# Two transformer layers on one core: neighbouring stages run into each other at the borders of attention, and the barriers between stages wait by part of the memory

## The chip, the cores and the metric

The kernel runs on one core of a Trainium2 chip. The metric is the device time of one execution in microseconds. TensorE is called PE here, with its weight loads as PEld, VectorE DVE, ScalarE ACT, GpSimd POOL, and SyncE SP; SP issues nearly all DMAs.

## The reference

The input x is 2 batches of 1024 tokens of 512 numbers, in float32. Six stages follow, each adding to x what it computes from a normalised x:

```python
x = x + 0.5 * L0_ffn(layernorm(x))   # hidden 1536, weights rounded to fp8, scales per column
x = x + L0_attn(layernorm(x))        # 16 query heads, 4 key/value heads of 32, biases, rope, causal
x = x + 0.5 * L0_ffn(layernorm(x))
x = x + 0.5 * L1_ffn(layernorm(x))   # hidden 2048
x = x + L1_attn(layernorm(x))        # 16 heads of 32, causal
x = x + 0.5 * L1_ffn(layernorm(x))
```

A feed-forward stage is `down(silu(gate(h)) * up(h))`; an attention stage is q, k, v, the causal softmax of q k / sqrt(32), times v, and the output projection.

## The kernel before

x stays in SBUF as 16 tiles of 128 tokens, and a chunk `c` is four tiles. Products in full precision are made from a high and a low part of each operand, in two or three passes. The stages are s = 0 to 5, of the kinds f0, a0, f0, f1, a1, f1.

**One plan sets every order.** `make_plan()` writes one list of steps, such as `("gu", s, g, c, m)` (gate and up products of one block of 128 hidden columns, group g, chunk c), `("down", s, g, c, i)` (down product of one token tile), `("ln_stats" / "ln_norm" / "ln_tp" / "ln_lo", s, t)` (the norm of tile t: statistics on DVE and POOL, the normalised tile `tmp` on ACT, four transposes on PE, high part on ACT, low part on DVE), `piece` and `piece_out` (256 tokens of q or k of four heads), `stack` (three DMAs that stack the parts of one head's q or k for the score products), `row` (scores by query, for the row maxima), `m_tp` and `m_lo` (the maxima transposed and sent by two `mrow` DMAs into the stacked q), `key` (scores by key), `pv` (times v), `take`, `y_turn`, `y_fin`, `y_tp` (the heads' results turned into `yT`), `oproj` (output projection). Each engine's program walks the same list and issues its share of each step in that order, with waits on semaphores that earlier steps raise; no engine reorders anything. Helper objects of the class `Beside` interleave jobs (norms, weights) with the main steps, one piece of a job at each `tick`. The PSUM bank of each step is chosen from the plan by `bank_turns`.

**A feed-forward stage** (`ffn`) loops over groups g (4 of f0, 8 of f1) and the four chunks. A chunk has MTS gate/up steps: three for f0 (16 products of 512 columns each) and two for f1 (24 products each). The down steps of a chunk, four tiles of six products, come one chunk later. `silu`, `prod` and the high part `a` are made by ACT and DVE, the low part by `a_lo` on DVE. In f0, down results go through `dso` (DVE) and are added to x by POOL; in f1, DVE adds them.

**An attention stage** (`attention`) first makes eight pieces (q and k of the first four heads), then the eight stacks, the v products, and 13 row steps ahead of the first key step; after that, row, key and pv steps and the products of the next heads run interleaved.

**Borders.** Between stages stands a step `begin`, at which ACT, DVE, POOL and SP each wait until all of x is complete, because the tiles of the new stage lie on memory of the old one:

```python
def begin(s):
    if s:
        on.wait_ge(*x_done(s - 1, NT - 1))
        all_kept(on)
```

SP's `begin` also issues small loads after that wait: three scale loads for f0; two rope tables, three bias columns and `bo` for a0. PE has no `begin`; it waits for what each step reads. `w_read` says when a weight's place may be overwritten.

The borders between feed-forward and attention are called A (stage 0 to 1, at 299 to 356 us of the span), B (1 to 2, at 804 to 844), C (3 to 4, at 1614 to 1666) and D (4 to 5, at 2157 to 2203).

## Time and profile before

| what | value |
|---|---|
| median of 3 runs | 2704.14 us (2702.6 to 2717.95) |
| the profiled execution | 2707.04 us, span 2705.3 us |
| PE busy | 2620.1 us, 97% of the span |
| DVE, ACT, POOL busy | 1368.5, 1078.1, 637.4 us (51%, 40%, 24%) |
| TensorE's clock, mean | 0.993 of 2.4 GHz |

The chip's profiler recorded one execution. Busy times don't add up to the span, since the engines work side by side; only the time in which PE has no work, or works at half clock, can be read as a loss where PE is the engine that everything ends on. Times in the text are microseconds from the start of the span.

### The profile page before, as it was taken

The page shows a single profiled execution, that of the slowest core. Times are in us where ns is not written, and L with a number is a line of the kernel's source. Part 1 is how long each engine was busy: PE and PEld are TensorE (multiplying, and loading weights), DVE is VectorE, ACT ScalarE, POOL GpSimd, SP SyncE. Part 2 cuts the span into 40 slices and gives each one's busy share as a digit, 9 for nine tenths or more (in the row PEclk, how much of TensorE's full clock was granted, in tenths as well). Part 3 has the DMA queues.
Part 4 walks back from the last instruction along what each step waited for, and adds up shares of the span by engine and source line. Part 5 has one row for each costly group of instructions (what it writes and reads, how often), then busy time and mean ns, then how long its engine had stood idle before and what let it go on. Part 6 is the DMA issues. An engine that isn't in the chain of part 4 may idle for free.

```text
span 2705.3 us, 36133 instructions
## 1 busy us (share of the span) xinstructions
PE 2620.1 (97%) x13216; PEld 1999.4 (74%) x13216; DVE 1368.5 (51%) x2784; ACT 1078.1 (40%) x1989; POOL 637.4 (24%) x1102
## 2 busy tenths in 40 slices
PE   6999899999999999999999999999999999999999
PEld 4788766666657888888888888666766588888887
DVE  7787566756655445533333344566356543333333
ACT  7555355655563223311211133556455632111111
POOL 3333432332222234411111121222122321111110
PEclk9999999999999999999999999999999999999999
DMA  4222121122111110000000002322132100000001
GB/s 144 71 71 74 39 65 33 36 56 48 36 37 52 35 43 9 31 24 24 24 26 29 24 9 64 86 60 61 37 81 62 43 32 24 26 29 24 24 16 63
DMA packets 59679, 119.80 MB, mean 44 GB/s; under 512 B 11632, under 2 KB 12656, under 8 KB 59504
## 3 DMA queue, kind: packets, MB, share of 16 engines
q1 hardware_dynamic: 59504, 117.51, 15.1%
q8 instruction: 105, 1.72, 0.3%
q14 instruction: 70, 0.57, 0.1%
HBM read 62.42 MB, written 13.63 MB: 28 GB/s over the span
## 4 chain that ended last, share of the span: by engine, by line
PE 82%; DVE 3%; issue 2%; ACT 2%; DMA 2%; POOL 2%; SPq 1%; DVEq 0%; ACTq 0%; POOLq 0%
PE psum L741 62%; PE psum L862 9%; PE psum L826 5%; PE psum L844 4%; PE psum L750 1%; DVE s1a0masked L1203 1%; PE psum L872 1%; DMA raw<-in_o 1%; DVE s4a1masked L1203 1%; POOL x L1312 0%; PE psum L882 0%; SPq L1399 0%; DVE tmp L1173 0%; ACT s4a1e L1032 0%; POOL rstd L1290 0%
## 5 line engine op out<-in xcount | busy, mean ns | idle before, releaser
L741 PE MATMUL psum<-hA_hi,wmem 128*128 128x256 f32 (+1 forms) x1536 | 404.0, 335 | 1.1 <-DVE s1a0negmax L1203 0.8
L741 PE MATMUL psum<-hA_lo,wmem 128*128 128x512 f32 (+1 forms) x864 | 294.2, 341 | 0.0
L741 PEld LDWEIGHTS psum<-hA_hi,wmem 128*128 128x128 f32 x1536 | 269.5, 191 | 32.9 <-DVE s1a0negmax L1203 1.8
L1032 ACT ACTIVATE s1a0e<-psum,p_scale 128x384 f32<-128x384 f32 (+5 forms) x384 | 203.5, 579 | 103.6 <-PE psum L844 102.5
L1032 ACT ACTIVATE s4a1e<-psum,p_scale 128x384 f32<-128x384 f32 (+5 forms) x384 | 204.7, 580 | 99.8 <-PE psum L844 97.7
L1203 DVE CUSTOM_DVE_ANT_0 s4a1masked<-psum,mask_q 128x512 bf16<-128x512 f32 (+7 forms) x256 | 189.9, 751 | 93.8 <-PE psum L826 91.0
L1203 DVE CUSTOM_DVE_ANT_0 s1a0masked<-psum,mask_q 128x512 bf16<-128x512 f32 (+7 forms) x256 | 189.5, 752 | 64.6 <-PE psum L826 62.3
L1155 DVE SCALAR_TENSOR_TENSOR x<-psum,x 128x512 f32<-128x512 f32 x256 | 175.5, 688 | 86.1 <-PE psum L741 81.9
L1126 DVE TENSOR_TENSOR s5f1prod<-psum,s5f1silu 128x512 f32<-128x512 f32 x64 | 44.3, 692 | 299.0 <-PE psum L741 299.0
L1126 DVE TENSOR_TENSOR s3f1prod<-psum,s3f1silu 128x512 f32<-128x512 f32 x64 | 44.3, 692 | 294.5 <-PE psum L741 294.5
L741 PE MATMUL psum<-s3f1w,s3f1a 128*128 128x512 f32 x768 | 181.1, 391 | 0.9 <-POOL s3f1w L1302 0.9
L741 PE MATMUL psum<-s5f1w,s5f1a 128*128 128x512 f32 x768 | 180.2, 390 | 0.9 <-POOL s5f1w L1302 0.9
L741 PEld LDWEIGHTS psum<-hA_lo,wmem 128*128 128x128 f32 x864 | 165.2, 191 | 19.7
L741 PEld LDWEIGHTS psum<-s5f1w,s5f1a 128*128 128x128 f32 x768 | 144.0, 188 | 31.7 <-DVE s5f1prod L1126 1.1
L741 PEld LDWEIGHTS psum<-s3f1w,s3f1a 128*128 128x128 f32 x768 | 143.8, 188 | 31.6 <-DVE s3f1prod L1126 1.1
L1328 POOL TENSOR_SCALAR_AFFINE_SELECT s4a1e<-s4a1e 128x128 f32<-128x128 f32 x256 | 74.5, 292 | 358.1 <-ACT s4a1e L1032 357.6
L1302 POOL TENSOR_TENSOR wmem<-raw,wmem 128x512 fp32r<-128x512 f32 x58 | 74.2, 1289 | 328.3 <-ACT wmem L933 328.3
L1328 POOL TENSOR_SCALAR_AFFINE_SELECT s1a0e<-s1a0e 128x128 f32<-128x128 f32 x256 | 74.9, 294 | 319.1 <-ACT s1a0e L1032 318.9
L862 PE MATMUL psum<-s4a1e,s4a1v 128*33 128x512 f32 (+7 forms) x1024 | 149.1, 413 | 0.1
L862 PE MATMUL psum<-s1a0e,s1a0v 128*33 128x512 f32 (+7 forms) x1024 | 148.6, 412 | 0.1
L826 PE MATMUL psum<-s1a0kst,s1a0qst 96*128 96x512 f32 (+4 forms) x384 | 126.7, 389 | 19.5 <-DVE s1a0negmax L1203 12.6
L826 PE MATMUL psum<-s4a1kst,s4a1qst 96*128 96x512 f32 (+4 forms) x384 | 124.6, 383 | 6.9 <-DVE s4a1negmax L1203 4.1
(196 smaller groups left out, 5066.5 us busy)
## 6 DMA issues: line engine op xcount, KB each, us to landing
s1a0qst<-s1a0qs SPq DMA_DIRECT2D x96, 128.0 KB, 2.4
s4a1qst<-s4a1qs SPq DMA_DIRECT2D x96, 128.0 KB, 2.4
s4a1kst<-s4a1ks SPq DMA_DIRECT2D x96, 128.0 KB, 2.4
raw<-in_gate SPq DMA_DIRECT2D x44, 256.0 KB, 2.7
raw<-in_up SPq DMA_DIRECT2D x44, 256.0 KB, 2.7
raw<-in_down SPq DMA_DIRECT2D x44, 256.0 KB, 2.7
rounded<-s0f0w SPq DMA_DIRECT2D x24, 256.0 KB, 2.0
s2f0w<-rounded SPq DMA_DIRECT2D x24, 256.0 KB, 5.0
```

The costliest lines, as they stand in the source:

```text
L741: ins = pe.matmul(out_, w, m, start=n == 0, stop=n == len(terms) - 1)
L750: ins = pe.transpose(ps[:, 0, k * P:(k + 1) * P], buf[:, k * P:(k + 1) * P], ident[:])
L826: ins = pe.matmul(ps[:, z, 0:pw], q_st[0:STACK, j, i * P:(i + 1) * P], k_st[0:STACK, j, z * pw:(z + 1) * pw], start=True, stop=True)
L844: pe.matmul(ps[:, 0, 0:pw], k_st[0:STACK + 2, j, jt * P:(jt + 1) * P], q_st[0:STACK + 2, j, q0 + z * pw:q0 + (z + 1) * pw], start=True, st ...
L862: ins = pe.matmul(psum[c * HALF:c * HALF + VW, bank, jt * HALF:CH], v[:, jt, kv, :], e[:, :, c, :], start=jt == 0, stop=jt == ST - 1, skip ...
L872: ins = pe.transpose(ps[:, 0, i * P:i * P + HALF + VW], ysb[:, i * P:(i + 1) * P], ident[0:HALF + VW, 0:HALF + VW])
L1032: act.activation(T[s]["e32"][:, begin_ + z * pw:begin_ + (z + 1) * pw - skip], src, ACT.Exp, bias=p_scale[:]).then_inc(sem["exp"], 1)
L1126: dve.tensor_tensor(prod[:], psum[:, bank, :], silu[:], ALU.mult).then_inc(sem["prod"], 1)
L1155: dve.scalar_tensor_tensor(x[:, tile, :], src, 0.5, x[:, tile, :], ALU.mult, ALU.add).then_inc(sem["x_add"], 1)
L1203: dve.tensor_tensor_reduce(T[s]["masked"][turn % 2][:, 0:width].rearrange("p (z w) -> p z w", **bare), scores, mask_q[:, SEQ - width:SEQ]. ...
L1302: pool.tensor_tensor(lo, buf[:], hi.bitcast(F32), ALU.subtract).then_inc(sem["w_lo"], 1)
L1328: pool.affine_select(out=block, in_=block, compare_op=ALU.is_ge, fill=0.0, base=0, pattern=[[1, P]], channel_multiplier=-1).then_inc(sem[" ...
```

## The change

No product is added or taken away. The plan changes at the four borders, and so does what `begin` waits for.

**Into attention (A, C).** The feed-forward stage doesn't issue the down steps of its last two chunks; it hands these eight steps to `attention` as `left`. There `begin` stands before them, and one down step is put between the last norm steps, the pieces, the first v products and the first rows. The memsets `v_ones` and `k_ones` come with `begin`, ahead of most of these.

**Out of attention (B, D).** `begin` and the gate/up steps of the next stage's first chunk (`first_products`) are put among the last steps of attention, at the ticks `EARLY_AT` of the loop that ends with y_turn, y_tp and oproj. The norms of tiles 8 to 15 then run two at a tick in the second chunk.

**The barriers.** `begin` waits for `gave_way(s)`: into attention, for the last up product and the last a_lo of the stage before; out of attention, for the last key product, row maximum, v output and bias add; between two feed-forward stages, for x as before. A second step, `open`, waits for x in attention, behind the first 13 rows but for the last. The tiles of each stage are laid out in another order and with a filler of 8192 numbers a partition, so that what is used early lies on what is free early. `w_read` uses `gave_way` for down weights, for group 1 and for v.

```diff
+EARLY_AT = (0, 1, 4, 7, 8)
+LATE_DOWNS = 2
+GAP = 8192
...
+    def first_products(s):
+        mts = MTS[STAGES[s]]
+        steps = [[("begin", s)]]
+        for m in range(mts):
+            steps.append([("gu", s, 0, 0, m)] + [("a_lo", s, 0, 0, m - 1)] * (m > 0))
+        return steps + [[("a_lo", s, 0, 0, mts - 1)]]
...
     def ffn(s):
...
-        plan.append(("begin", s))
+        after_heads = s > 0 and not is_ffn(s - 1)
+        if not after_heads:
+            plan.append(("begin", s))
...
         def tick(point):
-            norms.tick(NORMS_AT[kind][point])
+            norms.tick(2 if catching_up else NORMS_AT[kind][point])
...
+                catching_up = after_heads and (g, c) == (0, 1)
...
-        down(*pending)
+        left = []
+        if into_heads(s):
+            weights.finish(last_weight[s, groups - 1, "down"])
+            left = [[[("down", s, groups - 1, c, i)]] for c in (NC - 2, NC - 1) for i in range(CT)]
+        else:
+            down(*pending)
         weights.flush()
-
-    def attention(s):
+        return left
+
+    def attention(s, left):
         grouped = STAGES[s] == "a0"
-        norms.flush()
         plan.append(("begin", s))
+        downs = Beside(plan)
+        downs.waiting += left
+        while norms.busy(last_norm[s, 0]):
+            norms.tick()
+            downs.tick()
         plan.append(("v_ones", s))
         plan.append(("k_ones", s))
...
         while first.waiting or first.running:
-            first.tick()
+            norms.tick()
+            if norms.busy(last_norm[s, 1]) and any(("piece", s, 0, "q", 2) in job[0]
+                                                   for job in first.waiting[:1]):
+                first.tick(0)
+            else:
+                first.tick()
             v_weights.tick()
+            if len(downs.waiting) > LATE_DOWNS:
+                downs.tick()
...
+            if u % 2 == 0:
+                downs.tick()
         side.flush()
+        downs.flush()
+        plan.append(("open", s))
...
+        early = first_products(s + 1)
         for unit in behind:
             times_v(*unit)
-        side.flush()
+        ticks = 0
+        while side.waiting or side.running:
+            side.tick()
+            if early and ticks in EARLY_AT:
+                plan.extend(early.pop(0))
+            ticks += 1
+        for steps in early:
+            plan.extend(steps)
...
+        def gave_way(s):
+            p = s - 1
+            if s == 0:
+                return []
+            if not is_ffn(s):
+                m = MTS[STAGES[p]] - 1
+                g = GROUPS[STAGES[p]] - 1
+                return [(sem["up"], at("up", "gu", p, g, NC - 1, m)),
+                        (sem["a_lo"], at("a_lo", "a_lo", p, g, NC - 1, m))]
+            if is_ffn(p):
+                return [x_done(p, NT - 1)]
+            free = [(sem["s_k"], at("s_k", "key", p, HEADS_ALL - 1, ST - 1, 0)),
+                    (sem["row_max"], at("row_max", "row", p, HEADS_ALL - 1, LAST_ROW)),
+                    (sem["v_out"], at("v_out", "v_out", p, 1, 1 if p == 1 else ST - 1))]
+            return free + ([(sem["x_pool"], at("x_pool", "bias_x", p, 1, ST - 1))] if p == 1
+                           else [])
...
                 if g == 1 or name == "down":
-                    return [x_done(p, NT - 1)] if s else []
+                    return gave_way(s)
...
-            return [x_done(p, NT - 1)]
+            return gave_way(s) if name == "v" else [x_done(p, NT - 1)]
...
+            def open_(s):
+                on.wait_ge(*x_done(s - 1, NT - 1))
+
             def begin(s):
+                for free in gave_way(s):
+                    on.wait_ge(*free)
                 if s:
-                    on.wait_ge(*x_done(s - 1, NT - 1))
                     all_kept(on)
```

How the instructions move is shown at three places. The line numbers are those of each kernel.

VectorE at A, before: the last down results of stage 0 (`dso`), the low parts of norm tiles (`hA_lo`), then the piece outputs (`tmp` with the bias and rope tables, and the low part of `qs` or `ks`).

```order
L1150 SCALAR_TENSOR_TENSOR s0f0dso0<-psum,s0f0ds 128x512
L1150 SCALAR_TENSOR_TENSOR s0f0dso1<-psum,s0f0ds 128x512
L1080 TENSOR_TENSOR hA_lo<-psum,hA_hi 128x4x128
L1150 SCALAR_TENSOR_TENSOR s0f0dso0<-psum,s0f0ds 128x512
L1150 SCALAR_TENSOR_TENSOR s0f0dso1<-psum,s0f0ds 128x512
L1080 TENSOR_TENSOR hA_lo<-psum,hA_hi 128x4x128
L1150 SCALAR_TENSOR_TENSOR s0f0dso0<-psum,s0f0ds 128x512
L1150 SCALAR_TENSOR_TENSOR s0f0dso1<-psum,s0f0ds 128x512
L1173 SCALAR_TENSOR_TENSOR tmp0<-psum,s1a0bcol,s1a0ropeq 128x256
L1178 TENSOR_TENSOR s1a0qs1<-tmp0,s1a0qs0 128x256
L1173 SCALAR_TENSOR_TENSOR tmp1<-psum,s1a0bcol,s1a0ropek 128x256
L1178 TENSOR_TENSOR s1a0ks1<-tmp1,s1a0ks0 128x256
```

The same place after the change:

```order
L1184 BN_AGGR meanvar<-stats 128x2
L1264 SCALAR_TENSOR_TENSOR s0f0dso0<-psum,s0f0ds 128x512
L1194 TENSOR_TENSOR hA_lo<-psum,hA_hi 128x4x128
L1287 SCALAR_TENSOR_TENSOR tmp0<-psum,s1a0bcol,s1a0ropeq 128x256
L1292 TENSOR_TENSOR s1a0qs1<-tmp0,s1a0qs0 128x256
L1264 SCALAR_TENSOR_TENSOR s0f0dso1<-psum,s0f0ds 128x512
L1194 TENSOR_TENSOR hA_lo<-psum,hA_hi 128x4x128
L1287 SCALAR_TENSOR_TENSOR tmp1<-psum,s1a0bcol,s1a0ropek 128x256
L1292 TENSOR_TENSOR s1a0ks1<-tmp1,s1a0ks0 128x256
L1264 SCALAR_TENSOR_TENSOR s0f0dso0<-psum,s0f0ds 128x512
L1287 SCALAR_TENSOR_TENSOR tmp0<-psum,s1a0bcol,s1a0ropeq 128x256
L1292 TENSOR_TENSOR s1a0qs1<-tmp0,s1a0qs0 128x256
```

The first piece output stands behind one down result of the last two chunks, where eight stood before it, and from there down results and piece outputs alternate.

PE at C, before: down products of chunk 2 (`s3f1w` with `s3f1a`), then the transposes of norm tiles 4 and 5, and more down products.

```order
L741 MATMUL psum<-s3f1w210,s3f1a00 128x512
L741 MATMUL psum<-s3f1w211,s3f1a00 128x512
L741 MATMUL psum<-s3f1w210,s3f1a01 128x512
L741 MATMUL psum<-s3f1w210,s3f1a00 128x512
L741 MATMUL psum<-s3f1w211,s3f1a00 128x512
L741 MATMUL psum<-s3f1w210,s3f1a01 128x512
L750 MATMUL psum<-ident,tmp0 128x128 x4
L750 MATMUL psum<-ident,tmp1 128x128 x4
L741 MATMUL psum<-s3f1w210,s3f1a00 128x512
L741 MATMUL psum<-s3f1w211,s3f1a00 128x512
```

After the change, from the end of the last gate/up step (`s3f1hB` with `s3f1w`) on:

```order
L847 MATMUL psum<-s3f1hB0,s3f1w110 128x512
L847 MATMUL psum<-s3f1hB1,s3f1w110 128x512
L847 MATMUL psum<-s3f1hB0,s3f1w111 128x512
L856 MATMUL psum<-ident,tmp0 128x128 x4
L856 MATMUL psum<-ident,tmp1 128x128 x4
L847 MATMUL psum<-hA_hi,wmem 128x256
L847 MATMUL psum<-hA_lo,wmem 128x256
L847 MATMUL psum<-hA_hi,wmem 128x256 x2
```

The transposes follow the last gate/up products directly, ahead of the first pieces (`hA_hi` with `wmem`); all down products of chunk 2 stand behind them.

ScalarE at D, before: the last result of the heads (`ysb`), the two copies into `yT`, then silu and the high part `a` of the next stage's first chunk.

```order
L1032 ACTIVATE s4a1e32<-psum,p_scale 128x128
L1040 ACTIVATE s4a1ysb1<-psum 97x512
L1049 ACTIVATE s4a1yT0<-psum 128x8x64 x2
L969 ACT_TABLE_LOAD
L969 ACTIVATE s5f1silu0<-psum 128x512
L976 ACTIVATE s5f1a00<-s5f1prod0 128x512
L969 ACTIVATE s5f1silu1<-psum 128x512
L976 ACTIVATE s5f1a00<-s5f1prod1 128x512
```

After the change:

```order
L1150 ACTIVATE s4a1ysb1<-psum 97x512
L1079 ACT_TABLE_LOAD
L1079 ACTIVATE s5f1silu0<-psum 128x512
L1086 ACTIVATE s5f1a00<-s5f1prod0 128x512
L1079 ACTIVATE s5f1silu1<-psum 128x512
L1086 ACTIVATE s5f1a00<-s5f1prod1 128x512
L1159 ACTIVATE s4a1yT0<-psum 128x8x64 x2
```

Both gate/up steps of the first chunk have their silu and `a` ahead of the two yT copies.

## Rows read from the trace of the kernel before

**Rows 1.** The page, part 1: busy time and share of TensorE
```profile
PE 2620.1 (97%) x13216; PEld 1999.4 (74%) x13216; DVE 1368.5 (51%) x2784; ACT 1078.1 (40%) x1989; POOL 637.4 (24%) x1102
```

**Rows 2.** Windows of PE at A, B, C, D: stretch, length, busy, PEclk, DMA
```profile
298.76:352.20 53.44, 40.35 (x216) 0.87 0.35 89
...
804.70:843.95 39.25, 34.30 (x153) 0.91 0.24 88
...
1614.50:1666.00 51.50, 50.73 (x280) 1.00 0.34 83
...
2157.30:2202.30 45.00, 41.50 (x196) 0.92 0.07 24
```

**Rows 3.** Windows of PE over stretches at 1.2 GHz, same columns
```profile
331.60:345.20 13.60, 8.25 (x23) 0.50 0.80 177
...
352.10:355.50 3.40, 3.30 (x13) 0.50 0.00 0
...
809.50:812.90 3.40, 3.39 (x8) 0.50 0.00 0
...
829.90:833.30 3.40, 3.24 (x10) 0.51 0.09 33
...
2161.10:2167.90 6.80, 5.79 (x14) 0.50 0.00 0
```

**Rows 4.** Timeline of DVE at the last a_lo of stage 0: start, length, engine, line, tiles
```profile
299.69 1.47 DVE L1136 TENSOR_TENSOR s0f0a<-s0f0prod,s0f0a 128x512 fp32r<-128x512 f32 x2
```

**Rows 5.** Timelines at A: start, length, engine, line, tiles [idle before <-releaser]
```profile
300.82 0.81 ACT L914 ACTIVATE tmp<-x,shift,rstd 128x512 f32<-128x512 f32 x1
...
315.32 0.33 SPq L1361 DMA_DIRECT2D s1a0ropeq<-in_rope  x1
...
315.57 3.51 POOL L1320 MEMSET s1a0kst<- 2x4096 f32 x1
...
322.54 0.48 DVE L1173 SCALAR_TENSOR_TENSOR tmp<-psum,s1a0bcol,s1a0ropeq 128x256 f32<-128x256 f32 x1 [9.04 <-DMA s1a0bo<-in_bo]
...
332.30 1.88 SPq L1399 DMA_DIRECT2D s1a0qst<-s1a0qs  x3
...
349.25 1.70 SPq L1409 DMA_DIRECT2D s1a0qst<-s1a0mrow  x2
...
352.20 1.19 PE L844 MATMUL psum<-s1a0qst,s1a0kst 98*128 98x512 f32 x2 [1.22 <-DMA s1a0qst<-s1a0mrow]
```

**Rows 6.** The chain that ended last, in order of time: start, length, what
```profile
403.21 1.45 PE psum L741 x12
...
836.36 3.66 PE psum L741 x16
```

**Rows 7.** Timelines of PE and ACT at B
```profile
809.51 7.32 PE L741 MATMUL psum<-s1a0ow,s1a0yT 128*128 128x512 f32 x24 [1.57 <-DVE s1a0yT L1239]
...
823.37 1.28 ACT L966 ACT_TABLE_LOAD   x1 [14.75 <-DMA s2f0ds<-in_dscale]
...
830.06 1.12 PE L750 MATMUL psum<-ident,tmp 128*128 128x128 f32 x4 [2.34 <-ACT tmp L914]
```

**Rows 8.** Timelines of PE and ACT at C
```profile
1614.51 2.88 PE L741 MATMUL psum<-s3f1w,s3f1a 128*128 128x512 f32 x12
...
1616.03 1.51 ACT L914 ACTIVATE tmp<-x,shift,rstd 128x512 f32<-128x512 f32 x2
```

**Rows 9.** Timelines of ACT, PE and DVE at D
```profile
2160.13 1.08 ACT L1049 ACTIVATE s4a1yT<-psum 128x512 fp32r<-128x512 f32 x2 [2.06 <-PE psum L882]
...
2162.11 8.50 PE L741 MATMUL psum<-s4a1ow,s4a1yT 128*128 128x512 f32 x24 [1.57 <-DVE s4a1yT L1239]
...
2195.08 2.99 PE L741 MATMUL psum<-s5f1w,s5f1a 128*128 128x512 f32 x12 [0.90 <-POOL s5f1w L1302]
...
2201.53 1.03 PE L750 MATMUL psum<-ident,tmp 128*128 128x128 f32 x8
...
2202.80 1.29 DVE L1080 TENSOR_TENSOR s5f1hB<-psum,s5f1hB 128x512 fp32r<-128x512 f32 x2 [0.35 <-ACT s5f1hB L925]
```

More of the change, by code:

```diff
@@ L60, in is_ffn, with into_heads @@
     return STAGES[s][0] == "f"
+def into_heads(s):
+    return s + 1 < len(STAGES) and not is_ffn(s + 1)
 def names_of_group(s, g):
@@ L305, in make_plan @@
         weights.tick()
+    left = []
     for s in range(len(STAGES)):
-        (ffn if is_ffn(s) else attention)(s)
+        if is_ffn(s):
+            left = ffn(s)
+        else:
+            attention(s, left)
     return plan
@@ L494, in build, with weights_of @@
-                    t["silu"] = [sbuf(sc, f"{tag}silu{i}", [P, CH]) for i in range(2)]
-                    t["prod"] = [sbuf(sc, f"{tag}prod{i}", [P, CH]) for i in range(2)]
-                    if kind == "f0":
+                    t["w"] = [[None] * 3, [None] * 3]
+                    def weights_of(n, b):
+                        t["w"][b][n] = [wflat[:, (n * parts + p) * wn:(n * parts + p + 1) * wn]
+                                        if b == 0 and n < 2 else
+                                        sbuf(sc, f"{tag}w{n}{b}{p}", [P, wn], F32R)[:]
+                                        for p in range(parts)]
@@ new lines, in h_of, with gated, a_of @@
+                    def h_of():
+                        t["hB"] = [sbuf(sc, f"{tag}hB{p}", [P, KT, SEQ], F32R) for p in range(2)]
+                    def gated():
+                        for n in ("silu", "prod"):
+                            t[n] = [sbuf(sc, f"{tag}{n}{i}", [P, CH]) for i in range(2)]
+                    def a_of():
+                        t["a"] = [[sbuf(sc, f"{tag}a{b}{p}", [P, mts, CH], F32R)
+                                   for p in range(2)] for b in range(2)]
+                    if into_heads(s):
@@ L497, in build @@
                         if s == 0:
                             t["q_sets"] = [rounding_set(sc, f"{tag}{i}") for i in "abc"]
+                        h_of()
+                        for n, b in ((0, 0), (1, 0), (0, 1), (1, 1), (2, 0)):
+                            weights_of(n, b)
+                        gated()
+                        if kind == "f1":
+                            sbuf(sc, f"{tag}gap", [P, GAP])
+                        weights_of(2, 1)
+                        a_of()
+                    else:
+                        a_of()
+                        gated()
+                        for n, b in ((0, 0), (1, 0), (2, 0), (0, 1), (1, 1), (2, 1)):
+                            weights_of(n, b)
@@ L499, in build @@
+                    if kind == "f0":
                         t["gs"] = sbuf(sc, f"{tag}gs", [P, HIDDEN[kind] // P])
@@ L502, in build @@
                         t["dso"] = [sbuf(sc, f"{tag}dso{i}", [P, D]) for i in range(2)]
+                    if not into_heads(s):
+                        if kind == "f1":
+                            sbuf(sc, f"{tag}gap", [P, GAP])
+                        h_of()
                 else:
@@ L1059, in vector_program, with open_ @@
             on = Waits(dve)
+            def open_(s):
+                on.wait_ge(*x_done(s - 1, NT - 1))
             def begin(s):
+                for free in gave_way(s):
+                    on.wait_ge(*free)
                 if s:
-                    on.wait_ge(*x_done(s - 1, NT - 1))
                     all_kept(on)
@@ L1348, in sync_program, with open_ @@
             on = Waits(sp)
+            def open_(s):
+                on.wait_ge(*x_done(s - 1, NT - 1))
             def begin(s):
+                for free in gave_way(s):
+                    on.wait_ge(*free)
                 if s:
-                    on.wait_ge(*x_done(s - 1, NT - 1))
                     all_kept(on)
```

76 lines of the change are left out of this document (40 added, 36 removed).

## The prediction, on record before the changed kernel ran

> **What bounds the kernel now.** The page first: the matmul engine is busy 97% of the span [rows 1], so only its idle time and the time at its lower clock can be saved; what the other engines wait for costs nothing by itself. The idle time of the first 40 us (loading and first norms) is not touched. Next, the four places where the change acts, taken as windows [rows 2]: A, feed-forward into attention (stage 0 to 1), B, attention into feed-forward (1 to 2), C (3 to 4) and D (4 to 5). Window minus busy time gives PE's idle time: A 13.1, B 4.95, C 0.8, D 3.5 us. Then the stretches at 1.2 GHz instead of 2.4 [rows 3]: half of the busy time in them is lost, A 8.25/2 + 3.30/2 = 5.8, B (3.39 + 3.24)/2 = 3.3, D 5.79/2 = 2.9 us. So the places hold A 18.9, B 8.3, C 0.8, D 6.4, in all **34.3 us**, 1.3% of the kernel. That is the ceiling of this change: no product is added or removed, the change only moves work into gaps. Prices of the moved work: 16 products of 512 columns 3.66 us, a piece of q or k 1.45 [rows 6], two down tiles (twelve products of 512) 2.88 [rows 8].
>
> **A, before: a chain that PE doesn't set.** PE waits for a bias activation, then for the first stacking DMA. Both come from one cause: VectorE could start the eight piece outputs only at 322.54, after 9.04 us of waiting for the bias tables, whose six loads SP issued only when x was complete (from 315.32, bo landed last) [rows 5]. The outputs end about 332.3, where SP starts the first of eight stack issues (three DMAs, 1.9 us each, 15.3 us in all); then come the two mrow DMAs at 349.25 and the first key product at 352.20 [rows 5].
>
> **A, after.** SP's begin now waits for the last up product and last a_lo instead of x. VectorE's last two a_lo end at about 301.2 [rows 4], so the loads are issued some 14.1 us earlier and the tables land at about 308.3. I followed each engine's queue in the new order from 298.76 on:
> - PE reaches the transposes of tile 5 at once, with no down tiles ahead of them. ScalarE's normalised tile is written from 300.82 to 301.63 [rows 5]; PE idles 2.5 us. New gap.
> - ln_tp 7 now stands behind the 3.51 us memset of kst on GpSimd [rows 5], which the change puts ahead of that tile's statistics: normalised tile at about 309.7, PE there at 308.2, 1.6 us idle. New gap.
> - From there PE alternates pieces and down tiles without a wait (the banks that it wants were emptied earlier): q3 ends near 322.9, k3 near 324.4. VectorE, which takes a piece output in 1.3 us and a down tile in 0.7, finishes q3 at about 325.0. So the stacks start at **325.0 instead of 332.3**, 7.3 us earlier.
> - The stacks occupy SP until 340.3. The mrow DMAs came 1.7 us after the last stack issue before, since the row maxima were late (half clock, VectorE). Now the maxima can be ready at 338.7 at full clock, 342 with one or two half-clock stretches of 3.4 us. First key product at 343.2 to 347.3, against 352.2: **4.9 to 9.0 us gained, I take 7.5**, near the end without a delay, because SP's queue and not PE sets that end. A half-clock stretch after the first new gap would pass through to the stacks (1.7 us), and the stretch that now follows the first key product (1.65) may vanish: bounds 3.2 to 10.6.
>
> The Trainium skill (DMA: Bandwidth & Descriptors, Anatomy of one DMA) puts a fixed cost of about 2.0 us on a DMA of the other issue path; by that figure the last link of this chain, 2.95 us here from the mrow issue to the key product, would be an estimated 0.9 us shorter, and no term above uses it.
>
> **B.** Before, 4.95 us idle: the y transposes wait for their inputs, the output projection 1.57 us for yT, and the first transposes of the second half 2.34 us for a normalised tile; both times the clock fell [rows 3, 7]. ScalarE waited 14.75 us for the scale tables until 823.37 and then loaded a table [rows 7]. After: the scale loads are issued when the last key product is done (800.8), land at 806.6; silu 0 follows at 807.9, before gate and up of the first group end on PE (808.8). Gate/up 1 and 2 (3.66 us each) stand between y_turn, y_tp and oproj; yT is complete at about 816.3 and oproj's turn comes at 817.2. Statistics for tile 8 start after the next product group, and ln_norm 8 is done at 832.4 for transposes at 833.6. All waits are covered, by margins of 0.8 to 1.2 us; at transposes 10 and 11 I count 0.5 us idle. Cover gone altogether, 2 to 3 us would come back. Gain 8.3 - 0.5, with the small unexplained issue gaps of this place some 0.9 more: **8.7, bounds 6 to 9.3**.
>
> **C.** Here there was almost nothing to gain (0.8 us, waiting for the split value weights, which now come 7 us earlier: gained). But the transposes of tiles 4 and 5 again move ahead of two down tiles. Their inputs are written from 1616.03 to 1617.54 [rows 8]; PE is free at about 1614.7, where the down tiles began before. It idles 2.25 + 0.35 us and 0.2 at tile 7: 2.8 lost. So C **loses 2.0 us**; with a half-clock stretch 3.7.
>
> **D.** In this stage a chunk has two gate/up groups, not three, so nothing stands between y_tp and oproj, and ScalarE does the a copy of group 1 before the yT copies. y_tp starts at 2168.95; the product is taken up at 2169.35, a copy to 2170.7, and the oproj follows 1.98 us after the first yT copy as before (2160.13 to 2162.11 [rows 9]), at 2172.6. PE idles 2.6 us instead of 1.57. The gap of 0.76 and 0.27 us before it is covered by gate/up; the 0.90 us wait for down weights [rows 9] becomes 1.5, as both splits now stand behind two tiles' statistics on GpSimd. And the third chunk's gate/up follows directly on the transposes of tiles 10 and 11: from such a pair's start to its second low half takes 2201.53 to 2204.09 = 2.56 us [rows 9], minus 0.8 of the transposes, 1.75 idle, before covered by later transposes and downs. New losses 2.6 + 1.5 + 1.75 = 5.9 against 6.4, of which 2.9 was clock. At full clock D gains 0.5 (by end times on PE 1.4); one half-clock stretch takes 1.7. **Taken 0, bounds -2.5 to +1.4.**
>
> **The clock.** A single gap of 2.34 us (827.7 to 830.06) was followed by 3.4 us at half clock [rows 3, 7]; each such stretch costs 1.7 us. New gaps of 2.5, 2.6 and 2.6 us stand at A, C and D. I count one such price, split over C and A: 0.9 on C and the rest in A's 7.5. The Trainium skill (TensorE: Matmul & The Clock Gate, What's actually happening) calls the ramp penalty under 1% of a typical span and varying from run to run, and advises against fitting it; by that the clock would be left out of the sum, an estimated 16 us gain. The rows show it at three of the four places, so it stays in.
>
> **Sum.** 7.5 + 8.7 - 2.9 + 0 = **13.3 us** gained. The profiled execution took 2707.04 us (span 2705.3), the median of three is 2704.14, within the spread of 2702.6 to 2717.95: 2704.1 - 13.3 = **2690.8**. Ends of the terms together: 3.2 + 6 - 3.7 - 2.5 = 3 and 10.6 + 9.3 - 2 + 1.4 = 19.3, so 2685 to 2701.
>
> **Rivals.**
> - *All gaps filled*: the new gaps don't appear (ScalarE and GpSimd run earlier than I follow them) and 27 to 34 us go: 2674. For it: 18.9 us at A alone. Against: the tile 5 input can't be there before 301.6, whatever PE does, and SP needs 15.3 us for the stacks. 12%.
> - *The change doesn't free anything*: some engine's begin still waits for an event as late as x, or the bias tables land late because six loads queue with others. Then VectorE stops at the first piece output with down tiles behind it, and each place stays as it is: 2704. Against: both events of the new wait are done by 301.2. 10%.
> - *The clock trap, slower than before*: at A the clock stayed low for 13.6 us although PE was busy in the last part [rows 3]. If a stretch as long (6.8 us of loss) follows each new gap at A, C and D, A gains 9.0 - 6.8 = 2.2, C loses 8.8, D loses 5.4, B gains 8.7: 3.3 us slower, 2707. It decides when low stretches average over about 10 us. Against: elsewhere they are 3.4 and 6.8 us, since dense products follow, as they do behind all new gaps. 8%.
> - *Forecast*, 3 to 19 us faster: 70%.
>
> One per cent (27 us, and about what measurements of this kernel can tell from no change) is reached only in the first rival. The range takes in the second rival and the lower half of the first: 2677 to 2706. Faster by over 1%: 0.11; within: 0.86; slower: 0.03, a clock trap that lasts longer than any seen.
>
> **What the profile after would show.** First stack issue about 7 us earlier against the last gate/up of stage 0, and the bias wait gone. PE waits for ScalarE's tmp of about 2.5 us at both attention entries. B without a wait over 0.5 us. A wait of 2.6 us ahead of oproj only in the last attention. Wrong if the wait for tables stays, if PE finds a full bank behind a down tile, or if the first gaps at A and C are missing.

## The result, and the profile of the changed kernel

| kernel | median, us | runs | range |
|---|---|---|---|
| before | 2705.45 | 12 | 2700.77 to 2717.95 |
| changed | 2697.43 | 12 | 2694.97 to 2701.43 |

The ratio is 0.9973, 95% interval 0.9963 to 0.9984: the change gains **7.3 us** (4 to 10) where 13.3 were forecast. (By the medians alone it would be 8.0 us.) Timed once more, beside three of the experiments, the changed kernel gave 2696.83 us and a ratio of 0.9965 (0.9952 to 0.9977), 9.5 us. The direction was right, the size was not. The profiled execution took 2701.43 us, the longest of the twelve and 5.6 less than that of before, with a span of 2699.7 us. Its page says, where [rows 1] stood before:

```profile
PE 2616.3 (97%) x13216; PEld 1996.2 (74%) x13216; DVE 1367.8 (51%) x2784; ACT 1079.3 (40%) x1989; POOL 638.1 (24%) x1102
```

The four places as windows, with the columns stretch, length, then the busy time of PE, PEld, DVE, ACT and POOL, then the granted clock, the DMA share and GB/s. They answer to [rows 2]; A and C run between the same instructions as there, B and D hold more, since work of the next stage is among theirs:

```profile
299.33:345.37 46.04, 36.57 (x217) 30.75 (x215) 29.85 (x61) 11.75 (x22) 17.38 (x18) 0.99 0.41 104
793.00:845.28 52.28, 51.84 (x275) 40.65 (x272) 29.49 (x55) 26.86 (x45) 15.48 (x34) 1.00 0.19 66
1601.00:1656.10 55.10, 52.84 (x281) 45.53 (x281) 23.84 (x52) 15.62 (x30) 11.06 (x12) 0.97 0.32 77
2148.60:2207.00 58.40, 52.19 (x238) 42.35 (x233) 26.62 (x49) 20.57 (x33) 13.51 (x28) 0.94 0.06 19
```

Length minus PE's busy time: idle at A 9.5 us (13.1 before), at B 0.4 (4.95), at C 2.3 (0.8), at D 6.2 (3.5). Four of the stretches at half clock (1.2 GHz, granted clock 0.50) lie at these places (same columns; [rows 3] before):

```profile
344.80:351.60 6.80, 6.23 (x24) 5.99 (x25) 3.30 (x12) 4.31 (x7) 1.05 (x3) 0.50 0.00 0
1604.30:1607.70 3.40, 3.40 (x17) 3.40 (x17) 1.95 (x4) 2.53 (x4) 2.89 (x8) 0.50 0.46 154
2164.10:2167.50 3.40, 3.40 (x9) 2.64 (x9) 1.66 (x3) 0.00 (x0) 0.00 (x0) 0.50 0.00 0
2194.80:2198.20 3.40, 3.40 (x9) 2.67 (x9) 0.04 (x1) 0.51 (x1) 1.54 (x5) 0.50 0.24 77
```

Two more, of 3.4 us each, lie inside the attentions, at 713.4 and 1887.6; before there were also two such, at 720.7 and 1710.6.

**A** in the timeline (start, duration, engine, line, names, and in brackets the idle time before it with what ended it). The bias wait is gone; the two foretold gaps ahead of transposes are there, and the sync engine starts the stacks 6.1 us earlier than in [rows 5]:

```profile
302.24 0.66 PE L856 MATMUL psum<-ident,tmp 128*128 128x128 f32 x4 [2.31 <-ACT tmp L1024]
...
310.44 0.66 PE L856 MATMUL psum<-ident,tmp 128*128 128x128 f32 x4 [1.45 <-ACT tmp L1024]
...
326.21 1.89 SPq L1521 DMA_DIRECT2D s1a0qst<-s1a0qs  x3
...
342.68 1.44 SPq L1531 DMA_DIRECT2D s1a0qst<-s1a0mrow  x2
...
345.37 1.19 PE L950 MATMUL psum<-s1a0qst,s1a0kst 98*128 98x512 f32 x2 [1.48 <-DMA s1a0qst<-s1a0mrow]
```

**C and D**, same view; compare [rows 8] and [rows 9]:

```profile
1603.43 1.73 PE L856 MATMUL psum<-ident,tmp 128*128 128x128 f32 x8 [2.21 <-ACT tmp L1024]
...
2163.93 7.32 PE L847 MATMUL psum<-s4a1ow,s4a1yT 128*128 128x512 f32 x24 [2.47 <-DVE s4a1yT L1353]
...
2183.73 3.00 PE L847 MATMUL psum<-s5f1w,s5f1a 128*128 128x512 f32 x12 [1.59 <-POOL s5f1w L1420]
...
2193.38 7.38 PE L847 MATMUL psum<-s5f1hB,wmem 128*128 128x512 f32 x24 [2.14 <-DVE s5f1hB L1194]
```

Every foretold gap stands where it was put, within 0.4 us of its size: 2.21 at C against 2.25; 2.47, 1.59 and 2.14 at D against 2.6, 1.5 and 1.75. In B no wait of over 0.5 us is left. The waits are not what the forecast got wrong.

**The lead, place by place.** The same instruction is found in both traces by counting; its start in the kernel before, minus its start in the other, is that kernel's lead, and what the lead gains from one mark to the next is what the stretch is worth. Marks, by their time in the kernel before: the 11th pair of tile transposes (298.76, start of A), the 25th row product (358.13, end of A), the last 32 pv products of attention 1 (800.69), the 25th pair of tile transposes (1060.60, behind B), the 25th row product of attention 4 (1670.46, end of C), the last but one 32 pv products of attention 4 (2144.59), the end of the span. The median and the ratio are timed; the places of each row come from one profile:

| kernel | median, us | ratio to before (95%) | start | A | att. 1 | B | C | att. 4 | D | sum |
|---|---|---|---|---|---|---|---|---|---|---|
| forecast | 2690.8 | | 0 | 7.5 | 0 | 8.7 | -2.9 | 0 | 0 | 13.3 |
| changed | 2697.43 | 0.9973 (0.9963 to 0.9984) | -0.6 | 6.1 | 0.3 | 7.8 | -3.8 | -1.2 | -2.9 | 5.6 |
| same_again | 2696.83 | 0.9965 (0.9952 to 0.9977) | -0.7 | 6.6 | 1.6 | 7.8 | -3.8 | -1.4 | -2.8 | 7.4 |
| c_old | 2696.7 | 0.9973 (0.9962 to 0.9983) | -0.7 | 8.9 | -0.6 | 7.8 | 0.4 | -6.0 | -1.4 | 8.4 |
| d_old | 2696.84 | 0.9972 (0.9960 to 0.9984) | -0.4 | 6.9 | -0.9 | 7.8 | -2.3 | -2.7 | 2.8 | 11.3 |
| ac_old | 2695.0 | 0.9964 (0.9951 to 0.9977) | -0.8 | 7.9 | 1.8 | 7.8 | 0.1 | -1.8 | -2.9 | 12.1 |
| ac_filled | 2707.04 | 1.0012 (1.0002 to 1.0021) | -0.5 | 5.9 | -5.8 | 7.8 | 0.4 | -7.1 | -1.5 | -0.9 |
| filled_banks | 2695.33 | 0.9968 (0.9957 to 0.9979) | -0.4 | 7.6 | 1.7 | 7.8 | -1.1 | -2.0 | -1.2 | 12.4 |
| turned | 2716.23 | 1.0049 (1.0036 to 1.0061) | -0.4 | 3.4 | -7.7 | 7.8 | -5.1 | -5.7 | -1.3 | -9.2 |
| d_filled | 2689.25 | 0.9952 (0.9938 to 0.9965) | -0.2 | 8.9 | 1.6 | 7.8 | -3.8 | -0.5 | 6.6 | 20.4 |
| all_old | 2691.05 | 0.9956 (0.9944 to 0.9969) | -0.6 | 6.9 | 1.2 | 2.6 | -0.2 | 0.1 | 2.8 | 12.8 |
| b_new | 2696.94 | 0.9967 (0.9955 to 0.9980) | -0.5 | 7.3 | 2.1 | -1.1 | 0.3 | 2.3 | 1.1 | 11.5 |
| b_new_d_covered | 2697.54 | 0.9973 (0.9962 to 0.9984) | -0.4 | 9.6 | 1.2 | 0.5 | -0.1 | -0.9 | 1.2 | 11.0 |
| own_banks | 2685.44 | 0.9926 (0.9914 to 0.9939) | -0.4 | 7.5 | 1.3 | 7.8 | 0.0 | -1.2 | 6.6 | 21.6 |

Two profiles of the changed kernel agree by 0.2 us at B, C, attention 4 and D. The largest miss is D (0 forecast, -2.9). Attention 4, which had no term, cost 1.2 and 1.4; A, B and C each missed their term by 0.9 to 1.4.

### The profile page after: what moved, and what is told of

Read it like the earlier page. It is cut to its first block, busy times and chain, and to the rows that moved or that the text cites. A ratio compares the mean times of both kernels' runs of the same rounds, so it can differ in the third digit from the quotient of the medians.

```text
span 2699.7 us, 36151 instructions
## 1 busy us (share of the span) xinstructions
PE 2616.3 (97%) x13216; PEld 1996.2 (74%) x13216; DVE 1367.8 (51%) x2784; ACT 1079.3 (40%) x1989; POOL 638.1 (24%) x1102
## 3 DMA queue, kind: packets, MB, share of 16 engines
q1 hardware_dynamic: 59504, 117.51, 15.5%
## 4 chain that ended last, share of the span: by engine, by line
PE 85%; DVE 5%; ACT 3%; issue 3%; POOL 2%; DMA 1%; SPq 1%; DVEq 0%; ACTq 0%; POOLq 0%
PE psum L847 65%; PE psum L968 8%; PE psum L932 5%; PE psum L950 4%; PE psum L856 1%; SPq L1521 1%; DVE s1a0masked L1317 1%; PE psum L978 1%; DVE s4a1masked L1317 1%; DMA raw<-in_o 1%; POOL rstd L1408 0%; ACT tmp L1024 0%; DVE stats L1182 0%; PE psum L988 0%; DVE s0f0prod L1236 0%
## 5 line engine op out<-in xcount | busy, mean ns | idle before, releaser
L932 PE MATMUL psum<-s1a0kst,s1a0qst 96*128 96x512 f32 (+4 forms) x384 | 125.5, 385 | 18.9 <-DVE s1a0negmax L1317 13.1
```

Source lines behind the costliest of these rows:

```text
L932: ins = pe.matmul(ps[:, z, 0:pw], q_st[0:STACK, j, i * P:(i + 1) * P], k_st[0:STACK, j, z * pw:(z + 1) * pw], start=True, stop=True)
```

## Experiments

All are edits of the changed kernel's plan or of its bank table. The experiments ran on three chips, and kernels of different chips are compared by their ratio; the kernel before ran at 2703.67 us beside the first four, at 2704.62 beside the next four and at 2705.29 beside the last four.

### C in the old order: c_old

```diff
+ONE_BY_ONE = (4,)
-                if pending and not (into_heads(s) and (g, c) == (groups - 1, NC - 1)):
+                if pending and not (mixed(s) and (g, c) == (groups - 1, NC - 1)):
...
+        if s in ONE_BY_ONE:
+            norms.flush()
         plan.append(("begin", s))
```

`mixed(s)` is `into_heads(s)` without the stages of `ONE_BY_ONE`: these get no left down steps.

> The changed kernel with the old order of work at C alone (stage 3 finishes all its down tiles and all norms before attention 4 begins); A, B and D keep the new order, and the barriers by memory part stay everywhere. Theory (new gap plus its half-clock stretch): the matmul engine loses 2.2 us of waiting and 1.7 us of clock at C in the changed kernel, and between the last transposes of stage 3 and the first row products of stage 4 its lead over the kernel before fell from 13.8 to 10.0 us. With the old order that lead stays at 13 to 14 us, no half-clock stretch follows, and the time is 2697.4 - 3.7 = 2693.7 (ratio to the changed kernel 0.9986). Rival (given back later): the first heads of attention 4 are paced by other engines, so the lead saved at C is lost by head 2 and the time stays at 2697.4.

C did what the theory says, 0.4 instead of -3.8. The time did not follow: 2696.7 us, the ratio of the changed kernel. In this profile attention 4 lost 6.0 us, and 4.5 of them lie around one stretch of 6.8 us at half clock, from 1821.9. So neither theory is enough: C's loss is real, and something inside attention 4 is as large. What it is shows further down: with the order at C, the bank table of attention 4 changed too.

### D in the old order: d_old

```diff
-        after_heads = s > 0 and not is_ffn(s - 1)
+        after_heads = s > 0 and not is_ffn(s - 1) and s not in LATE_BEGIN
...
-        early = first_products(s + 1)
+        early = [] if s + 1 in LATE_BEGIN else first_products(s + 1)
```

`LATE_BEGIN` is `(5,)` here.

> The changed kernel with the old order at D alone (gate/up of stage 5 starts after the last output projection of attention 4). Theory (three new gaps of 2.5, 1.6 and 2.1 us and two half-clock stretches at 1.7 us each against 3.5 us of gaps and 2.9 us of clock before): D gives back its loss of 3.0 us, so 2697.4 - 3.0 = 2694.4, and the profile shows waits of 0.8, 1.6 and 0.9 us as before, with one stretch at half clock. Rival (chance of one profile): the loss at D stands in one profiled execution that was 4.0 us over the median of its kernel; then the timed median doesn't move, 2697.4, and the new profile shows D no better.

D went from -2.9 to +2.8 in the profile, 5.7 us, with the waits of the kernel before (1.6, 1.0 and 0.8 us) and no half-clock stretch at all, where the kernel before had one of 6.8 us. Its +2.8 over that kernel is this stretch, 2.9 us, and nothing of the order. The median again stayed within 1 us of the changed kernel's, where 3 were expected: unclear, since an effect of 3 us is about the width of the interval.

### A and C in the old order: ac_old

`ONE_BY_ONE = (1, 4)`.

> The changed kernel with the old order at A and C (all down tiles and norms before either attention begins), the new order at B and D, and the barriers by memory part everywhere. Theory (A is set by when the bias tables land and by the sync engine's queue of stack transfers, so the barrier alone gives A its gain): lead over the kernel before at the first key product of stage 1 stays 6 to 8 us, C gives back 3.7 us: 2693.7. Rival (the order gives A's gain: only down tiles between the pieces fill the matmul engine's wait): the lead at the first key product falls to 1 to 3 us and the time is 2697.4 + 5 - 3.7 = 2698.7.

A kept its gain without a single down tile between the pieces: 7.9 us by the table. The barrier, with the layout that belongs to it, made it and not the order. The median is 2695.0, toward the theory's 2693.7.

### Two down tiles ahead of the transposes: ac_filled

```diff
         downs.waiting += left
+        if s in (1, 4):
+            downs.tick(2)
```

> The changed kernel with two of the eight left down tiles put ahead of the transposes of tiles 4 and 5 at A and C (2.9 us of matmuls where the engine now waits 2.3 and 2.2 us); nothing else is moved. Theory (gap and clock): both waits go, at C with the half-clock stretch behind it: C gains 2.2 + 1.7 = 3.9 us; at A the sync engine's queue still sets the end, 0 to 1 us. 2697.4 - 4.4 = 2693.0. Rival (the wait moves): tiles 6 and 7 or the first piece outputs come later by as much, the gaps stand behind the down tiles and the clock falls there: 2697.4.

Slower than the kernel before: 2707.04 us, 14 us over the theory. At C the theory holds (0.4 instead of -3.8; no wait ahead of the transposes). At A the rival holds: the wait has moved behind the down tiles and is one of 3.8 us where there were two of 2.31 and 1.45 (waits of PE from 299 to 330: engine, tile, line waited for, total, times, longest):

```profile
PE psum L858 <- ACT tmp L1026: 3.8, 1, 3.8
```

But the 14 us are in neither place: the attentions behind lost 5.8 and 7.1 us. Nothing was moved inside them. What does change there is what the planner derives from the order: it gives each product the PSUM banks that, by the plan, were emptied longest ago. In this kernel 157 of 880 steps of stage 1 and 190 of 912 of stage 4 take their banks over from another step than in the kernel before; in the changed kernel these are 31 and 173.

### The same order with other banks, both ways: filled_banks and turned

```diff
-def bank_turns(plan):
+def bank_turns(plan, wanted={}):
...
         mine = list(range(first, first + width))
+        if step in wanted and max(empty[i] for i in wanted[step]) < now:
+            mine = wanted[step]
         banks[step] = mine
```

`wanted` is the table of the other kernel: filled_banks has the moved down tiles and the changed kernel's banks at every step, turned has the changed kernel's order and ac_filled's banks.

> The kernel of the run before with two down tiles put ahead of the first transposes at A and C, but with each step's PSUM banks taken from the table that the changed kernel itself has, so that every step takes its banks over from the same earlier step as there. It ran at 2707.0 where 2693.0 was expected, although C alone gained 4.3 us; inside the two attentions its lead fell by 5.1 and 7.1 us, where the changed kernel's fell by 0.4 and 1.2. Theory (bank order): the planner hands out PSUM banks by who emptied one longest ago, moving two down tiles turns that order for the whole attention behind them, and row products then wait for the row maxima of a later tile; with the old table the losses inside go and the gain at C stays: 2697.4 - 3 to 4 = 2694. Rival (the moved tiles themselves disturb the attention, by a later x or by the clock): still over 2703.

> The changed kernel with its order untouched on every engine, and only the PSUM banks of each step taken from the table of the kernel with two down tiles moved ahead (147 of 880 steps of stage 1 and 172 of 912 of stage 4 take over a bank from another step). Theory (bank order): 4 to 5 us of new waits for row maxima and exponentials inside stage 1, as much inside stage 4: 2697.4 + 9 = 2706, 2703 at least. Rival (the order of work made the loss, banks don't matter): 2697.4.

Both go as the theory says. filled_banks ran at 2695.33 with attention 1 back at +1.7 and attention 4 at -2.0 (at C it kept 2.7 of the 4.2 us; a wait of 1.2 for `hA_lo` had come up there); turned, with no instruction moved on any engine, at **2716.23**, 19 us over the changed kernel and 10 more than expected. Waits of PE in attention 1, from 488 to 705 us, turned first, then filled_banks:

```profile
PE psum L936 <- DVE s1a0negmax L1321: 7.9, 12, 1.7
...
PE psum L936 <- ACT s1a0e L1146: 1.1, 1, 1.1
```

```profile
PE psum L936 <- DVE s1a0negmax L1321: 5.8, 10, 1.3
```

A row product takes over the bank of a row whose maximum VectorE has not yet taken, or of exponentials that ScalarE is still reading. Here these waits are the smaller part of the loss. Windows of PE over the same work of attention 1 (stretch, length, busy, clock, DMA share, GB/s), in the same order:

```profile
486.44:693.91 207.47, 193.85 (x1161) 0.98 0.18 44
```

```profile
481.21:681.68 200.47, 189.69 (x1162) 1.00 0.19 46
```

Of the 7.0 us between them 2.8 are idle time and 4.2 are longer busy time, with 10.2 us at half clock in turned and none in filled_banks. In attention 4 the idle part can be read off one stretch, from the 56th to the 63rd 32 pv products of the kernel, with the same 611 matmuls in all kernels and full clock. Windows of PE (stretch, length, busy, clock, DMA share, GB/s) of before, changed, filled_banks, all_old, own_banks and turned:

```profile
2044.65:2144.59 99.94, 98.24 (x611) 1.00 0.21 52
```

```profile
2034.72:2136.02 101.30, 97.88 (x611) 1.00 0.21 51
```

```profile
2029.71:2131.03 101.32, 97.91 (x611) 1.00 0.21 51
```

```profile
2034.45:2134.59 100.14, 98.25 (x611) 1.00 0.21 51
```

```profile
2029.63:2129.58 99.95, 97.79 (x611) 1.00 0.21 52
```

```profile
2048.42:2152.41 103.99, 98.06 (x611) 1.00 0.21 50
```

Idle: 1.7, 3.4, 3.4, 1.9, 2.2 and 5.9 us. It goes by the bank table: the changed kernel, same_again, filled_banks, d_filled and d_old, which share the table there, all have 3.41 to 3.46; ac_filled has turned's, 5.9. So the changed kernel's own table costs it 1.7 us of idle time in this stretch, 1.4 by the length. That is the loss in attention 4 for which the forecast had no term.

The clock part is not mere chance either. From the 43rd to the 45th 32 pv products of the kernel, also in attention 4, nine profiles need 28.6 to 29.2 us at full clock. The five others need 31.8 to 33.7 us, and each has a stretch of 3.4 or 6.8 us at half clock there. These five have two tables that the nine do not have for their row, key and pv steps: c_old, ac_old and own_banks share one, ac_filled and turned the other. Changed, c_old, own_banks and turned:

```profile
1815.41:1844.10 28.69, 27.25 (x179) 1.00 0.29 72
```

```profile
1811.13:1844.51 33.38, 30.58 (x178) 0.90 0.26 64
```

```profile
1808.35:1840.51 32.16, 29.51 (x179) 0.95 0.25 64
```

```profile
1827.25:1860.92 33.67, 29.93 (x180) 0.90 0.24 59
```

In two pairs nothing but the table differs: turned against changed, 33.7 for 28.7, and ac_filled against filled_banks, 33.7 for 29.2. So a bank table can bring the clock down at the same place each time. Which of the small waits does it is open: the longest one ahead of such a fall was 1.1 us in c_old and 0.4 in ac_old.

### D covered: d_filled

```diff
-EARLY_AT = (0, 1, 4, 7, 8)
+EARLY_AT = {2: (0, 1, 4, 7, 8), 5: (0, 1, 4, 6, 6)}
...
+        if s == 5:
+            return steps + [[("a_lo", s, 0, 0, mts - 1)], [("gu", s, 0, 1, 0)]]
...
                 if after_heads and (g, c) == (0, 0):
                     weights.tick(2)
+                    if s == 5:
+                        weights.tick(0)
+                        norms.tick(2)
+                        norms.tick(2)
```

The first gate/up group of the second chunk now stands between y_tp and oproj; splits, statistics and norms follow oproj at once.

> The changed kernel with D alone ordered so that its three new gaps are covered: the first gate/up group of the second chunk stands between the y transposes and the output projection, both down weight splits and the statistics and norms of tiles 8 to 11 come before the second group of that chunk, and the third chunk's gate/up comes two down tiles after the transposes of tiles 10 and 11. Theory (gaps and what follows them): 2.5 + 1.6 + 2.1 us of waiting go, the stretches at half clock behind them mostly too, D gains 6 to 8 us: 2697.4 - 7 = 2690.4. Rival (other waits take their place, on x or on the tmp tiles): 1 to 3 us, 2695.

It came out within 1.2 us of the theory: 2689.25, and D at +6.6 instead of -2.9. Two stretches of PE that hold D, same columns as above:

```profile
2141.00:2202.00 61.00, 60.87 (x305) 1.00 0.09 29
2143.00:2195.00 52.00, 51.87 (x258) 1.00 0.05 16
```

0.13 us idle in 61, at full clock. So D's three waits and what follows them are worth 9.5 us between the two orders in these profiles, and the forecast's zero for D was not a property of the place. The timed runs show less: by the ratios d_filled is 3.5 to 5.7 us faster than the changed kernel.

### The barriers alone: all_old

`ONE_BY_ONE = (1, 4)`, `LATE_BEGIN = (2, 5)`. Its plan is the plan of before with only the two `open` steps added, so the order on every engine and each step's banks are as before; the memory layout and what `begin` waits for are the changed kernel's.

> The old order of work at all four places, with the memory layout and the barriers by memory part of the changed kernel. Theory: the barriers alone give A its 7 us (bias tables and stack transfers early), at B the scale tables and ScalarE's table load come early but the waits for yT and the first norms stay, 0 to 2 us, C 0.8, D 0: 2705.4 - 8.5 = 2697, as fast as the changed kernel. Rival (barriers and order act only together): 2704.

2691.05 us, 12 us faster than before by the ratio, nearly what was forecast for the whole change, and 2 to 5 us **faster than the changed kernel**. The ratio intervals, 0.9944 to 0.9969 against 0.9963 to 0.9984 and 0.9952 to 0.9977, overlap, so the sign by times alone is likely and not certain. The profile says the same by place: the new order adds 5.2 us at B and takes 3.6 at C, 1.3 in attention 4 and 5.7 at D. The last number leans on the clock: all_old, like d_old, had no half-clock stretch at D. Over all profiles the changed order at D stands between -1.2 and -2.9 (seven), the old one between 0 and +2.8 (four). A by the barrier alone, sync queue and first key product:

```profile
325.11 1.88 SPq L1533 DMA_DIRECT2D s1a0qst<-s1a0qs  x3
...
341.62 1.72 SPq L1543 DMA_DIRECT2D s1a0qst<-s1a0mrow  x2
...
344.60 1.19 PE L962 MATMUL psum<-s1a0qst,s1a0kst 98*128 98x512 f32 x2 [1.23 <-DMA s1a0qst<-s1a0mrow]
```

The stacks start 1.1 us earlier than with the down tiles between the pieces, presumably since VectorE doesn't have these to take.

### B new, D covered, and the banks once more: same_again, b_new, b_new_d_covered, own_banks

b_new is all_old with B's new order; b_new_d_covered adds d_filled's order at D; both take the banks of the kernel before wherever these are free by the plan. own_banks has the order of b_new_d_covered and the banks that the planner gives by itself.

> The changed kernel itself once more, on the chip and in the hour of the three kernels beside it, so that differences of 3 to 6 us are told from differences between chips: 2697.4 by every theory, and by the ratio 0.9973 again. A second profile also shows which half-clock stretches come back (theory: only how many there are is stable, about 9 us of cost over the whole kernel, and not their places; rival: the three behind the new gaps at A, C and D stand again in the same places).

> Memory layout and barriers of the changed kernel, the new order at B alone, the old order at A, C and D, and the PSUM banks of the kernel before (12 steps next to B take another). Theory (the terms add up by place): the kernel with the old order everywhere ran at 2691.05, and B's order is worth 7.75 instead of 2.6 us: 2691.05 - 5.1 = 2686. Rival (saved time at B is taken back inside the stages behind it): 2691.

> As the kernel with the new order at B alone, with D in the covered order too (the first group of the second chunk ahead of the output projection, splits and norms early), A and C old, PSUM banks of the kernel before. Theory: D in that order gained 6.6 us over the kernel before and 2.8 in the old order with the new barriers: 2686 - 3.8 = 2682. Rival (D's old order under the new barriers is as good, its 2.8 were the clock by chance): 2686.

> The same order of work as the kernel before it in this list (B new, D covered, A and C old), but with the banks that the planner hands out by itself (164 of 912 steps of stage 4 take over a bank from another step than in the kernel before the change). Theory (bank order): some of those steps are the row products, which wait for maxima and exponentials 1 to 3 us longer inside stage 4, as in the changed kernel (1.2 us): 2682 + 2 = 2684. Rival (this bank order is harmless, only that of the kernel with the moved down tiles is bad): 2682.

same_again: 2696.83, the same; of its stretches at half clock the one at C and the two at D come back within 3 us of their places (1602.3, 2162.1, 2192.8), the others not. The rival named there holds in this pair.

b_new and b_new_d_covered missed by 11 and 15.5 us, at B and the second at D too, where new work meets a bank table made for the old order. The timeline of b_new at B:

```profile
802.90 0.50 PE L871 MATMUL psum<-hA_hi,wmem 128*128 128x512 f32 x1 [2.45 <-DVE s1a0y L1367]
...
811.15 0.50 PE L871 MATMUL psum<-hA_hi,wmem 128*128 128x512 f32 x1 [1.84 <-DVE s1a0yT L1377]
...
835.55 3.02 PE L871 MATMUL psum<-s2f0w,s2f0a 128*128 128x512 f32 x12 [2.01 <-DVE s2f0hB L1218]
```

Gate/up products that depend on nothing of `y` wait for VectorE to read y out of the bank they were given. With the planner's banks the same order gives B 7.8 and D 6.6 us (own_banks), with the forced ones 0.5 and 1.2. The edit was wrong, not the theory of places. b_new_d_covered and own_banks have the same plan to the last step, so their 12 us are the third case in which the bank table alone makes the difference.

own_banks is the best kernel of the study: **2685.44 us**, ratio 0.9926 (0.9914 to 0.9939), 19.9 us faster than before and 11.4 faster than the changed kernel timed beside it. 2684 was expected. Its attention 4 lost 1.2 us, the size that the theory had. But it lost 3.2 us in the one stretch shown above, more by the clock than by waits, and regained 2.0 elsewhere, and the pair that was to show it by time was spoilt at B and D.

## Why the prediction missed its size

**The chain at A: right, and for its reason.** Stacks foretold at 325.0 came at 326.21, the first key product at 345.37 (343.2 to 347.3 foretold). Up to there 7.4 us were gained, counted from the start of A. Then the clock fell for 6.8 us around the key product, where it fell for 3.4 before; the forecast had let that stretch vanish or stay, not double. In the second profile it was 3.4 us there and 3.4 more from 332.6. The term measured 6.1 and 6.6 for 7.5. all_old and ac_old show that the barrier alone makes it.

**B: right, 7.8 for 8.7.** The "small unexplained issue gaps, some 0.9 more" did not come back: the idle time fell by 4.5 us, and the 6.8 us at half clock, which cost 3.3, went. It is 7.8 in all ten profiles that have this order with banks handed out for it.

**C: -3.8 for -2.9.** The gap was 2.21 us, and the half-clock stretch that followed cost its full 1.7 us, of which the forecast had counted 0.9. In d_old the same gap had no stretch behind it and C cost 2.3.

**D: the step that failed, -2.9 for 0.** The term that was mis-sized is the clock behind the new gaps, above all at D. The waits were right: "new losses" of 5.9 us measured 6.2. What was wrong is how the prediction went on: D gains 0.5 at full clock, one half-clock stretch takes 1.7, and 0 is taken. Both the first and the last gap were followed by 3.4 us at half clock, 3.4 us of loss. All in all the forecast put "one such price" on three new gaps of over 2 us at A, C and D, and overlooked that D's last, foretold at 1.75, would be a fourth. In the profiles of all kernels that have them, the gaps of 2.31 at A, 2.21 at C, 2.47 and 2.15 at D were followed by a stretch in 3 of 6, 4 of 5, 5 of 7 and 5 of 7 cases: two in three. Four gaps at 1.7 x 2/3 are 4.5 us, not 1.7. By that D comes to -1.8 (5.9 + 2 x 1.15 against 6.4) and the sum to about 11. This share is taken from the profiles afterwards and is no more exact than 25 cases make it. Attention 4 (1.3) and the late start (0.6) bring it to some 9 us, where 7.3 and 9.5 were timed.

**Attention 4: no term at all, -1.3.** The prediction followed the order on each engine and not the bank table that the same plan yields. What the table can do is the largest effect of the study: 19 us in turned, some 11 of them in waits, as the next section shows, and the rest at half clock. The 9 us expected there had no price for the clock.

**Start.** The changed kernel is 0.6 us late before A begins. All kernels with the new layout are, by 0.2 to 0.8; the cause was not tried.

**Rivals.** The clock trap of 6.8 us behind each gap did not come: only at A was there a stretch of that length. The barrier did free what the forecast said, so the rival that nothing is freed is out. "All gaps filled" is out by the gaps found.

## The clock, over all timed runs

Each timed run records its span and its mean granted clock, and span x (1 - clock) is what PE would get back at full clock throughout (too much by the idle time in such stretches; three decimals, so means only). Kernel before, the 45 runs beside the experiments: clock 0.9941, 16.0 us, and 2686.6 us without them. Changed kernel, all 17 runs: 0.9966, 9.0 us, and 2686.4 without them. **All of the measured gain is time at half clock**; the idle time saved at A and B (8.1 us) is spent at C, D and in attention 4 (5.9 by the windows) and by the late start. (Idle time inside half-clock stretches counts in both sums, so they don't add up exactly.) Without the clock's part all_old has 2679.4, d_filled 2680.2, own_banks 2675.9 and turned 2697.3 us. It also explains c_old: 2684.1 without the clock's part, 2.3 us better than the changed kernel, which is the gap at C, but 10.8 us of clock instead of 9.0. The old order saved the wait, and the clock took most of that back.

The Trainium skill (TensorE: Matmul & The Clock Gate, What's actually happening) calls the ramp penalty, the time at the lower clock until the engine is granted the full one, under 1% of a typical span, and different from run to run. Counted over the whole kernel, the runs agree with both: 16.0 of 2702.5 is 0.6%, and c_old's profile has stretches at 81.1, 303.0 and 552.2 where the changed kernel's has none. But 16.0 us is more than the gain that was at stake here, so for an edit of this size it can't be left out of a forecast; it has to stand in it as a chance for each gap.

## What to carry to other kernels

Ask of an overlap which part does the work, the barrier that lets go early or the new order: here the barrier, with its memory layout, probably gave more alone than with the new order (the layout was not tried by itself), and the change's order paid only at B, where what was moved really covered a wait; D paid once its order did so too. When a plan also derives something by rule (banks, buffers, slots), compare that table too, for every step behind the edit: a harmless looking move of two tiles changed it for the two attentions behind them and cost more than any gap. Put a price on each new gap of 2 us and more: its own length, and two thirds of the 1.7 us that a half-clock stretch costs. Then move independent products into it.

## What was not expected of the hardware

Gap and clock: in the 14 profiles, between 90 and 2690 us of the span, 31 waits of PE were 2.2 us or longer, and a stretch at 1.2 GHz began during the wait or within 4 us behind it in 22 of them. Of 19 waits of 1.8 to 2.2 us it was 9, of 44 of 1.4 to 1.8 us 8, of 56 of 1.0 to 1.4 us 19, of 273 waits of 0.6 to 1.0 us 15. So the chance is highest behind the longest waits but doesn't grow evenly with them; waits that stand close together are counted each for itself. The same gap in the same code (2.31 us at A) had one in c_old, d_old and d_filled and none in the changed kernel, twice. Stretches lasted 3.4 or 6.8 us, one 13.7.

That the choice of PSUM banks alone moves a kernel of 2700 us by 19 us, 0.7%, with the order of instructions unchanged on every engine, was not expected either: turned against the changed kernel, 1.0049 (1.0036 to 1.0061) against 0.9973 (0.9963 to 0.9984).
